# Gathering by source with one 256-column matmul where two neighbouring groups of nodes share a block

## The reference, cut to what matters

```python
def _L3_gnn_ref(x, edge_index, W1, b1, W2, b2):
    src, dst = (edge_index[0], edge_index[1])
    xs, xd = (x[src], x[dst])
    def reflection(a, b):
        h = jax.nn.relu(jnp.concatenate([a, b], axis=1) @ W1.T + b1)
        return h @ W2.T + b2
    def householder(v):
        vn = v / jnp.maximum(jnp.linalg.norm(v, axis=1, keepdims=True), 1e-12)
        return jnp.eye(d, dtype=v.dtype)[None] - 2.0 * vn[:, :, None] * vn[:, None, :]
    F_s = householder(reflection(xs, xd))
    F_d = householder(reflection(xd, xs))
    L_sd = -jnp.einsum('eki,ekj->eij', F_s, F_d)
    ...
    coef = deg_inv_sqrt[src] * deg_inv_sqrt[dst]
    msg_s = coef[:, None] * jnp.einsum('eij,ej->ei', L_sd, xd)
    msg_d = coef[:, None] * jnp.einsum('eji,ej->ei', L_sd, xs)
    out = x - jnp.zeros_like(x).at[src].add(msg_s) - jnp.zeros_like(x).at[dst].add(msg_d)
    return jax.nn.relu(out)
```

## Time and profile before

| | |
|---|---|
| median of 3 runs | 15562.0 us (15555.02 to 15573.69) |
| the profiled execution | 15625.38 us, span 15623.6 us |
| mean granted TensorE clock over the span | 0.824 |
| last stage, from its first turn to its last | 11687.05 to 15544.40 us, 3857.35 us |
| PE in that stretch | busy 3813.11 us, granted clock 0.96 |
| DVE in that stretch | busy 3494.88 us |
| matmuls of L2088 on `own` | 11478, 128 columns each |

### The profile page before, as it was taken

How to read it: one execution, slowest core, us unless ns; L and a number is a source line. 1 busy time by engine, 2 the same in 40 slices (tenths; PEclk the granted TensorE clock), 3 DMA queues, 4 the chain that set the end, 5 groups by cost and what they waited for, 6 DMA issues and landing times. The chain is left out here.

```text
span 15623.6 us, 474073 instructions
## 1 busy us (share of the span) xinstructions
PE 11688.2 (75%) x158466; PEld 9184.0 (59%) x158467; DVE 12468.0 (80%) x23402; ACT 7727.0 (49%) x17320; POOL 8206.3 (53%) x8491
## 2 busy tenths in 40 slices
PE   1344444444444388789999978878959999999998
PEld 1233333333333266578888856656648888888886
DVE  4577777777777588878888878878868999999997
ACT  2244444444444366556666646656635555555554
POOL 1777777777777799711111179989951111111111
PEclk9855555555555699999999989999989999999998
DMA  8233333333333377622222267767752222222222
GB/s 225 63 91 90 92 91 91 91 91 91 91 91 91 110 220 220 186 98 109 103 109 105 107 170 225 225 189 226 226 130 80 82 84 82 85 84 82 84 85 65
DMA packets 1742381, 1897.00 MB, mean 121 GB/s; under 512 B 1011017, under 2 KB 1449883, under 8 KB 1716987
## 3 DMA queue, kind: packets, MB, share of 16 engines
q1 hardware_dynamic: 1617117, 1853.32, 40.1%
q0 software_dynamic: 123008, 41.82, 1.7%
q10 hardware_dynamic: 2078, 0.15, 0.0%
HBM read 1445.12 MB, written 449.46 MB: 121 GB/s over the span
## 5 line engine op out<-in xcount | busy, mean ns | idle before, releaser
L637 POOL DMA_INDIRECT rec<-sort_ring,sort_idx x3712 | 3657.0, 985 | 1657.0 <-issue 1129.3
L1292 DVE TENSOR_TENSOR e_full<-e_feats,e_masks 128x1280 bf16<-128x1280 bf16 x3537 | 2787.5, 850 | 244.8 <-ACT e_feats L1249 218.1
L1192 PE MATMUL e_acc<-e_full,e_sel 128*128 128x384 bf16 (+1 forms) x11760 | 2120.4, 327 | 360.1 <-DVE e_full L1292 360.1
L1444 PE MATMUL e_acc<-e_outer,e_sel 128*128 128x272 f32 x7840 | 1896.1, 397 | 3.9 <-DVE e_outer L1539 3.9
L1247 ACT CAST e_masks<-e_kind 128x1280 bf16<-128x1280 fp8e4 x1179 | 1482.8, 1258 | 775.4 <-DVE e_full L1292 737.2
L753 PE MATMUL sort_ps_rows<-ident_h,sort_code 128*128 128x128 f16 x7840 | 1067.5, 308 | 1036.7 <-DVE sort_code L879 862.3
L1159 POOL TENSOR_SCALAR e_lo<-iota_b,e_src_lo 128x128 bf16<-128x128 bf16 x1470 | 1683.7, 1145 | 0.0
L1192 PEld LDWEIGHTS e_acc<-e_full,e_sel 128*128 128x128 fp8e4 x11760 | 1061.0, 97 | 1023.2 <-issue 387.0
L900 DVE TENSOR_SCALAR sort_made<-sort_rows_code,code_of 128x1664 fp8e4<-128x1664 f16 x882 | 1642.9, 1935 | 0.0
L1444 PEld LDWEIGHTS e_acc<-e_outer,e_sel 128*128 128x128 f32 x7840 | 1458.7, 190 | 282.0 <-issue 4.1
L1158 POOL TENSOR_SCALAR e_hi<-iota_b,e_src_hi 128x98 bf16<-128x98 bf16 x1470 | 1521.2, 1035 | 68.4 <-POOL e_src_lo L1154 64.1
(11 more groups left out here) (455 smaller groups left out, 27113.4 us busy)
## 6 DMA issues: line engine op xcount, KB each, us to landing
e_hot<-stream SPq DMA_DIRECT2D x888, 480.0 KB, 3.7
stream<-sort_made SPq DMA_DIRECT2D x98, 2568.0 KB
e_sel<-stream SPq DMA_DIRECT2D x1176, 160.0 KB, 2.5
e_st<-stream SPq DMA_DIRECT2D x99, 1888.0 KB, 7.3
sheaf_gather<-stream SPq DMA_DIRECT2D x393, 384.0 KB, 3.1
e_hot<-stream SPq DMA_DIRECT2D x294, 448.0 KB, 3.5
tail<-sort_made SPq DMA_DIRECT2D x98, 660.0 KB
sheaf_by_dst<-tail SPq DMA_DIRECT2D x491, 128.0 KB, 3.0
```

The lines of the kernel that those rows point to most:

```text
L637: nc.gpsimd.indirect_dma_start(out=rec[q], out_offset=bass.IndirectOffsetOnAxis(ap=idx[:, s, q, c:c + 1], axis=0), in_=ring[:, s, q, c, :] ...
L1192: last = mm(acc[h][:, 0:cols_all], now[:, n * P:(n + 1) * P], full[q & 1][:, n, :], start=j == 0, stop=j == NT - 1)
L1292: last = v.tensor_tensor(full[q & 1][:, :, 0:cols].rearrange("p j (t k f) -> p j t k f", t=TYPES, k=3)[:, :, :, k, :], feats[q & 1][:, :, ...
L1444: last = mm(acc[h][:, 0:cols], sel[q & 1][:, n, :], outer[q & 1][:, n, :], start=j == 0, stop=j == NT - 1)
```

## The change

In an even group `j` with a neighbour, the third of its blocks of nodes is the first block of group `j + 1`: `(5 * j >> 1) + 2` equals `5 * (j + 1) >> 1` for even j, which a new assertion states. Both hots lie side by side (`at`, `at + 1`) and so do the two groups' columns in `ps_xt`. The third matmul of the even group is made 256 columns wide and covers both, and the first matmul of the odd group is left out. Of the 39 groups, 38 form 19 pairs; group 38 stays alone, since its neighbour is SELF.

```diff
+assert all((5 * j >> 1) + SPREAD - 1 == 5 * (j + 1) >> 1 for j in range(0, GROUPS, 2))
...
                     for k in range(SUB):
                         j = s * SUB + k
                         spread = SPREAD if j < GROUPS else 1
+                        paired = j + 1 < GROUPS if k % 2 == 0 else j < GROUPS
                         for c in range(spread):
+                            if paired and k % 2 == 1 and c == 0:
+                                continue
+                            both = 2 if paired and k % 2 == 0 and c == SPREAD - 1 else 1
                             at = (first + k) * SPREAD + c
                             rows = own[:, (5 * j >> 1) + c, :] if j < GROUPS else own_side[:, K3:3 * K3]
-                            last = mm(ps_xt[0:2 * K3, k * P:(k + 1) * P], rows, now[:, at * P:(at + 1) * P], start=False,
+                            last = mm(ps_xt[0:2 * K3, k * P:(k + both) * P], rows, now[:, at * P:(at + both) * P], start=False,
                                       stop=c == spread - 1, skip_group_check=True)
```

## The result

The changed kernel takes 15670.56 us (median of 4 runs, 15653.82 to 15700.5) against 15561.97 (4 runs, 15555.02 to 15573.69): a ratio of 1.0070, 95% interval 1.0058 to 1.0082, so 109 us slower. The forecast was 15559, no change. Slower by over 0.2% had a chance of 0.27, and the range of 15480 to 15680 holds the time.

What follows compares the result with a forecast made beforehand. PE bounds the last stage, exchanging the pace with DVE; 12 pairs x 2.4 ns = 29 ns a block, x 98 = 2.8 us, off the 15562.0 us median gives 15559 us, range 15480 to 15680.

Steps and rivals of the forecast that it cites:

- the six turns that I put on the path: In each block, six of ten turns lie where PE leads; only their 12 pairs were to save time.
- What a pair is worth: In the L2088 matmuls, one 256-column matmul for two of 128 saves about 2.4 ns at full clock.
- Rival D: In the matmul stream, the weight load was the pace; each pair saves 56 ns, 66 us, 15496 us; chance 0.03.
- The sum: Over the stage's 98 blocks, 12 pairs x 2.4 ns = 29 ns a block, 2.8 us in all.
- drops: Stretches in the last stage where PE's clock falls from 2.4 to 1.2 GHz for 6.83 us, 40.96 us apart.
- the 63 us: Whole kernel: the runs' median, 15562.0 us, lies 63 us under the profiled execution's 15625.4; the same 3 us comes off.
- excess: Last stage's time over 98 free blocks of 37.90 us, from slow-clock stretches: 143 us, fifty times the forecast saving.
- B: In the last stage, slow-clock stretches become rarer; excess falls by a quarter to a half, 36 to 72 us; chance 0.25.
- C: Last stage's blocks settle on slow-clock stretches, or sequences last longer or gain extra 46.39 us blocks; around 15630 us; chance 0.27.
- a full lock: Every block of the last stage holds a slow-clock stretch and takes 40.96 us; excess 300 us instead of 143, 15716 us.
- drops as before: In the last stage, small gain with slow-clock stretches unchanged: 15559 us, own range 15531 to 15590; chance 0.45.
- The waits: PE's two waits for DVE in a free block, L2125's and the first L2131's, each grow 5 to 10 ns.

Runs made afterwards that it cites:

- the single fill: One zero-weight 512-column matmul in PE's wait after the tenth step: kernel before 15470.84 us; on another chip changed 19125.07 us, before 19123.43.
- the drops filled away: Three zero-weight 512-column matmuls per block, in both PE waits and at the loop's end: changed kernel 15472.1 us, kernel before 15470.0 us.
- the second profile: The changed kernel run again, unaltered, on another chip: 19340.77 us, ratio 1.0070 to the kernel before there.
- a fill at the loop's end: Kernel before plus one zero-weight 512-column matmul per block at the end of the loop over blocks: 15604.0 us, ratio 1.0015.

## Why the prediction was right or wrong

*What bounds the stage.* Right. PE and DVE hand the pace to each other, and the six turns that I put on the path are those whose saving shows: the free block takes 37.87 us with all pairs or with the 12 on the path, and 37.90 with the 7 under DVE.

*What a pair is worth.* Right: 2.4 ns forecast, 2.7 measured in the block. The start of the next matmul comes 109 ns after a wide one, against 109.7 from the line through 128 and 512 columns. The estimate from the Trainium skill ("TensorE: Matmul & The Clock Gate", section "Back-to-back issue gap"), with its rates of about 81 ns per matmul at 128 columns and 131 at 512, was a gain of 75 us. The trace doesn't agree, with 56 and 109 ns at 128 and 256 columns, and the measurement decides. Rival D had a gain of 66 us, which doesn't show either.

*The sum.* 29 ns a block forecast, 30 measured, 34 with the drops gone: 3 us, as put. Between 30 and 34 lies the loop's turn: from PE's last matmul before it to the first behind it there are 0.283 us in the changed kernel's free blocks against 0.278 before, and 0.279 in both kernels with the single fill (medians).

*The median against the profiled execution.* Wrong. I took the 63 us between them for a constant and subtracted the same 3 us from the lower one. By the subtraction above they were drops: the profiled execution had an excess of 143 us, a median run about 80. The prices of B and C mixed the two as well. Without any drop the time would be 15559 - 80 = 15479 us and not 15419, and the kernel before with one fill took 15471; a full lock would be 15779 and not 15716. Had I asked what makes two executions of one program differ by 0.4%, the spread of the excess would have been seen to be larger than the whole question.

*The clock.* Here the forecast fell. The step that failed is "drops as before" as the likeliest case, with 0.45, which left the excess out of the sum. In its place the runs show 12 blocks of 46.4 us where there were 5, a stage of 3904.69 us instead of 3857.35, and a median 109 us higher; with the drops filled away, 15472.1 against 15470.0 us, the loss is gone. I had shown that the excess was fifty times the sum and that a shift of 20 to 30 ns changes how drops slide through the blocks, and still put the most weight on no change of them. What happened is C in part. Its full form, a block locked to the 40.96 us between drops, did not come: as I said, it takes 40 ns, and the changed blocks of 41 us took 40.97 and more. Its second form, each sequence of 41 us blocks lasting for longer, did not show in the first profile, whose sequences have one to three; in the later one a few have four. Its third, an extra block of 46.39 us in each cycle, did: 5 became 12, and in the second profile 14, though the cycle is not the twelve blocks that I read into the rows. I had priced that at 69 us and C at 15630; the runs give 109 us. For B there was nothing.

*Which end is which.* The direction could not be had from the rows of before: a block 30 ns longer also loses (57 us). The kernel before had a block length between two bad ones, not at the end of a slope. That is argued from these three lengths; a finer scan of lengths was not run. Nor is length all of it: the changed kernel with one narrow matmul more has before's free block of 37.90 us and still takes 30 us more. What besides the length moves the drops is open.

*The waits.* Forecast to grow by 5 to 10 ns each; L2125's grew by 7, the other by about 4, under the forecast.

## What to carry to other kernels

When a loop's period is steady to a few nanoseconds and its clock drops now and then, count the drops before pricing an edit: here a block of 38 us made 30 ns shorter cost 109 us through them, and one made about 30 ns longer cost 57. Find the stretch of thin TensorE work ahead of the drops and try a matmul that changes nothing in each wait there, since which one matters had to be measured: one place took 0.67% off the kernel before (0.43% on the other chip), another nothing. On the first chip the runs then agreed within 13 us where they had differed by 50. A saving of 3 us stays out of reach of the medians even so; it is read from the length of a free block in the trace. And if a profiled execution lies 0.4% off the median of its runs, find out by what before taking the difference for a constant.

## What was not expected of the hardware

The drops came in two lengths, 6.8 us (a block of 41 us) and 20.5 us (one of 46.4), and in the one profile of it a fill at the loop's end left only the second kind. A matmul of 512 columns put into PE's wait for DVE let the scatter behind it start 50 ns earlier than it had without it (0.240 us after the last L2104 instead of 0.292). So not all of the 0.292 us had been DVE's; what the other 50 ns were is not shown. And one matmul of 16 columns lengthened a free block by 27 ns in the changed kernel and by 33 in the kernel before (medians), with some blocks at 37.99 us there, whose loop's turn is longer; why it isn't the same is open.
